# An attention kernel deals its queries to partitions in eights instead of fours

## What is computed

```
x = x + 0.5 * tanh(layernorm(x) @ W @ A1 @ A2 + bias)          # feed-forward
xn = layernorm(x) * ln_g + ln_b
q, k, v = xn @ Wq + bq, xn @ Wk + bk, xn @ Wv + bv             # (8, 1024, 16, 16)
p = pe @ Wp                                                    # (1024, 16, 16)
content = einsum("bihd,bjhd->bhij", q + u_bias, k)
pos     = einsum("bihd,jhd->bhij",  q + v_bias, p)
pos     = relative_shift(pos)     # pad one zero column, view (S+1, S), drop the first row
attn    = softmax((content + pos) * 16 ** -0.5)
x = x + einsum("bhij,bjhd->bihd", attn, v) @ Wo + bo
x = x + 0.5 * tanh(layernorm(x) @ W @ A1 @ A2 + bias)          # feed-forward
```

## Time and profile before

| what | us |
| --- | --- |
| median of 3 runs (lowest to highest) | 3821.3 (3819.82 to 3822.86) |
| the profiled execution, its own time | 3820.24 |
| its span, first to last instruction | 3818.5 |
| attention phase, first to last start of L724 | 518.8 to 3569.0 |
| PE busy, ACT busy, DVE busy, POOL busy | 3384.0, 2312.8, 1830.7, 1265.6 |
| bytes moved by DMA, mean rate | 1221.6 MB, 320 GB/s |

### The profile page before, as it was taken

How to read it: one execution, slowest core, us unless ns; L and a number is a source line. 1 busy time by engine, 2 the same in 40 slices (tenths; PEclk the granted TensorE clock), 3 DMA queues, 4 the chain that set the end, 5 groups by cost and what they waited for, 6 DMA issues and landing times. The chain is left out here.

```text
span 3818.5 us, 86185 instructions
## 1 busy us (share of the span) xinstructions
PE 3384.0 (89%) x24380; PEld 1856.3 (49%) x24380; DVE 1830.7 (48%) x3584; ACT 2312.8 (61%) x3252; POOL 1265.6 (33%) x1228
## 2 busy tenths in 40 slices
PE   3677579999999999999999999999999999999776
PEld 2445334444444444444444444444444444444565
DVE  3555324444444444444444444444444444444444
ACT  1222247666777666667677677666776667776322
POOL 1111023333333333333333333333333333333100
PEclk7888879999999999999999999999999999999888
DMA  2332489999999999999999999999999999999543
GB/s 82 110 110 96 161 283 376 374 374 373 375 375 371 375 372 370 372 373 375 372 376 374 373 373 373 376 374 374 374 374 371 375 374 374 374 375 376 163 115 88
DMA packets 467980, 1221.60 MB, mean 320 GB/s; under 512 B 92144, under 2 KB 176624, under 8 KB 467952
## 3 DMA queue, kind: packets, MB, share of 16 engines
q1 hardware_dynamic: 467952, 1221.25, 88.5%
HBM read 624.38 MB, written 596.65 MB: 320 GB/s over the span
## 5 line engine op out<-in xcount | busy, mean ns | idle before, releaser
L724 DVE CUSTOM_DVE_ANT_0 at_pos_in<-at_ps_con,at_pos_in 128x1024 f32<-128x1024 f32 x1024 | 1254.0, 1225 | 1606.4 <-PE at_ps_con L612 1425.8
L761 POOL TENSOR_SCALAR at_pos_in<-at_pos_in,at_neg_max 128x1024 f32<-128x1024 f32 x1024 | 1146.3, 1119 | 1908.1 <-DVE at_neg_max L724 1908.1
L692 ACT ACTIVATE at_pos_out<-at_ps_pos 128x1024 f32<-128x1024 f32 x1024 | 1049.4, 1025 | 629.8 <-PE at_ps_pos L612 629.8
L701 ACT ACTIVATE at_prob<-at_ps_turn 128x512 f32<-128x512 f32 x2048 | 1110.6, 595 | 362.2 <-PE at_ps_turn L635 362.2
L612 PE MATMUL at_ps_con<-at_right,at_left 32*128 32x512 f32 x4096 | 1156.2, 640 | 153.3 <-DVE at_neg_max L724 151.8
L612 PE MATMUL at_ps_pos<-at_right,at_left 32*128 32x512 f32 x4096 | 1163.8, 644 | 46.9 <-DMA at_right<-scratch_pos_rows 39.0
L635 PEld LDWEIGHTS at_ps_turn<-keep_ident,at_pos_in 128*128 128x128 f32 x8192 | 898.7, 143 | 627.0 <-issue 428.7
L635 PE MATMUL at_ps_turn<-keep_ident,at_pos_in 128*128 128x128 f32 x8192 | 1113.7, 279 | 1.4 <-POOL at_pos_in L761 0.2
L647 PE MATMUL at_ps_pv<-at_prob,at_v_aug 128*32 128x512 f32 x4096 | 545.3, 605 | 0.8 <-issue 0.8
L612 PEld LDWEIGHTS at_ps_con<-at_right,at_left 32*128 32x128 f32 x4096 | 308.2, 183 | 344.9 <-ACT at_pos_out L692 198.8
L658 PEld LDWEIGHTS at_ps_head<-keep_fold,at_head_T 128*128 128x128 f32 x2048 | 247.8, 191 | 195.7 <-DVE at_head_T L732 148.6
(11 more groups left out here) (82 smaller groups left out, 1357.6 us busy)
## 6 DMA issues: line engine op xcount, KB each, us to landing
scratch_scores<-at_pos_out SPq DMA_DIRECT2D x1024, 512.0 KB, 7.5
at_pos_in<-scratch_scores SPq DMA_DIRECT2D x1024, 512.0 KB, 7.7
at_left<-scratch_qk_rows SPq DMA_DIRECT2D x512, 64.0 KB, 5.2
scratch_qk_rows<-de_qk SPq DMA_DIRECT2D x48, 512.0 KB, 5.0
de_x<-in_L_attn_x_dram SPq DMA_DIRECT2D x16, 512.0 KB, 6.4
scratch_x<-de_x_bo SPq DMA_DIRECT2D x16, 512.0 KB, 3.0
scratch_values<-de_values SPq DMA_DIRECT2D x1, 8192.0 KB, 30.3
at_right<-scratch_pos_rows SPq DMA_DIRECT2D x256, 32.0 KB, 5.7
```

Of the source, the lines that this page charges most:

```text
L692: act.activation(pos_out[:, t.slot, :], ps_pos[:, :, :].rearrange("p a m -> p (a m)"), ACT.Copy)\
L701: act.activation(prob[t.t // QUAD % 2][:, 4 * n:4 * n + 4, k * P:(k + 1) * P], ps_turn[:, n, :].rearrange("p (j i) -> p j i", i=P), ACT.Exp)\
L724: dve.tensor_tensor_reduce(pos_in[:, t.slot, :], ps_con[:, :, :].rearrange("p a m -> p (a m)"), pos_in[:, t.slot, :], -SCALE, 3.0e38, ALU. ...
L761: pool.tensor_scalar(pos_in[:, t.slot, :], pos_in[:, t.slot, :], -1.0, neg_max[:, t.slot:t.slot + 1], ALU.mult, ALU.add).then_inc(shifted, 1)
```

## The change

`GAPS` becomes 8. Partition 8v + h now holds query v + 16h of the tile. The scratch tensors in DRAM hold the same values at the same places as before; only the way to and from partitions differs.

```
 STRIP = 32
-GAPS = 4
+GAPS = 8
 HALF = S // 2
```

## The result

The changed kernel takes 4409.2 us (4395.6 to 4416.8, four runs), the kernel before 3822.1 us beside it. The ratio is 1.153 with a 95% interval of 1.150 to 1.156: 15% slower, 587 us more. The forecast was 4435 us.

What follows compares the result with a forecast made beforehand. PE and its chain were taken to lead, the DMA engines just keeping up. Slower write and read-back add 0.60 us a tile, 614 us over 1024 tiles; with 0.4 us of L374 and 3820.2 us, 4435 us, range 3813 to 5150.

Steps and rivals of the forecast that it cites:

- What bounds before: Attention phase: PE and its chain lead at 2.975 us a tile, and the transfers just keep up.
- The engines have no idle time to use: Attention phase: transfers are always queued and the 16 engines never run dry, so 3% slower transfers find no idle time.
- Rival 1: Write and read-back cost the same in the new shape and PE goes on leading: 3821 us, 3815 to 3829; chance 0.28.
- L374 and the heads: Bias-and-copy of the q's costs 0.4 us more, median within 1150 to 1200 ns; the stores of the heads cost nothing.
- Transfers with an outer size of 16 cost the engines more: Write and read-back in 16 groups of 8: engines get in each other's way, up to 1.46 times as long.
- The terms of the sum: Engine time per tile: 3.04 us now, plus 0.44 for the read-back and 0.17 for the write, together 3.65 us.
- 1.12 for the write and 1.31 for the read-back: Factors on 1.43 us of each engine: smallest of three 64 KB loads for the write, their mean for the read-back.
- the DMA then sets the beat, and nothing hides it: Attention phase: a tile takes 3.58 us, 0.60 us over 2.98, in all 614 us for 1024 tiles.
- The signs named: Attention phase: GB/s from 374 to about 310, share near 1.02, read-back waits from 58.7 us to hundreds, PE's busy share falls.
- landings did not grow to 9 us: Sign for write and read-back: landings go from 7.5 us to 9 or more.

Runs made afterwards that it cites:

- light4: The kernel before with the read-back cut to the first 512 of 1024 columns; 3824.4 us against 3833.9.
- w4r8: The kernel before with only the read-back (with the content q and the heads) going by 16 groups of 8; 3990.1 us against 3833.5.
- extra64: The kernel before with one more write of 64 KB beside each tile's write, into a scratch that nobody reads; 4308.9 us, 475 us more than beside it.
- light8: The changed kernel with the read-back cut to the first 512 of 1024 columns; 4262.1 us.
- w8r4: The kernel before with only the write (and its q with the position bias) going by 16 groups of 8; 4537.2 us, timed again at 4527.7 us, ratio 1.179.
- after_lp: The changed kernel with its loads and the store of the heads issued by POOL instead of SP; 4369.6 us, 1.138 of the kernel before.

## Why the prediction was right, point by point

**What bounds before.** Right. PE's beat was read as 2.975 us and light4, without any wait for transfers, runs at 2.976.

**The engines have no idle time to use.** Right. In w4r8 a slower read-back made the tile 0.16 us longer with the share still at 1.02 and SP not full, so nothing hid it. Rival 1 falls with it, and with the write alone at 1.89 us. extra64, made for this point, did not settle it.

**L374 and the heads.** Right: 1167 ns, and the dense phase did not move.

**Transfers with an outer size of 16 cost the engines more.** Right, taken from three loads of 64 KB: alone, 16 groups of 8 took 1.95 us of each engine as a write and 2.11 as a read, where 32 groups of 4 took 1.28 and 1.52. The transfers one by one put the cost at the SBUF side and in both directions. That the engines get in each other's way there was my reading, and no run shows it. What rows 16 apart in DRAM cost is not separated for this very shape, but 8 groups of 16, with rows 8 apart, took no more (1.97 and 2.02 us).

**The terms of the sum.** Mis-sized, and in a way that cancelled: that 4435 us came so near to 4409 is luck. The step that took 1.12 for the write and 1.31 for the read-back failed: alone they measure 1.52 and 1.39. In the mix the single edits cost (4281.8 - 519.2) / 1023 - 2.98 = 0.70 us a tile for the write, where 0.17 was forecast, and 0.16 us for the read-back, where 0.44 was (0.43 at a share of 1.02). The reason given, that reading SBUF had no row and so should suffer less, was a choice without evidence. Nor would the true ratios of transfers alone have helped: with 1.52 and 1.39 the same sum gives (3.04 + 1.43 x 0.52 + 1.43 x 0.39) / 1.02 = 4.26 us a tile, some 5130 us, since in the mix the shapes cost less than alone. The sum for both, 3.58 us a tile, met 3.543 only because the two together cost less than the write alone.

**What nobody had in the account: SP.** The prediction named SP's queue nowhere, although it holds all 26 issues of a unit in order. In light8 it is what binds. In the changed kernel SP and the engines are both full (33.2 us of waits for ACT on SP, a share of 1.00 on the engines). So the step "the DMA then sets the beat, and nothing hides it" is half of what the runs show, and a rate that counted the engines alone came out near.

**The signs named.** GB/s went to 314 (about 310 forecast), the share to 1.00, the waits for the read-back to 1670.8 us, PE's busy share fell from 89% to 80%, and the granted clock from 1.00 to 0.97 in the attention phase. One sign failed: landings did not grow to 9 us but stayed at 7.3 us in the median for the write. The likely reason is that SP is held up at the issue, so that the time goes into the issues and not into the landings: in w4r8, where no issue grew, they did reach 9.0 and 9.3 us.

**Open.** Why both shapes together (4409 us) are faster than the write's alone (4528 us). The engines' time for a tile is nearly the same, 1.00 x 3.543 = 3.54 and 0.97 x 3.678 = 3.57 us, so what differs is idle time of the engines, 3% of the tile in w8r4. SP has next to none in either, and its issues of a unit are 1.4 us longer in w8r4, about the 1.1 us by which the unit is longer; so the difference passes through SP's issues. Why these are held up longer when the read-backs are the fast ones, no run tests. Open too is which of SP and the engines would bind the changed kernel if the other were free; after_lp with its loads placed earlier would tell. And open is what exactly an issue waits for when it is held up.

## What to carry to other kernels

A regrouping of rows on the DRAM side of a transfer is not neutral although bytes, rows and instructions stay the same: here the time went with the size of the outermost dimension. For a tile of 128 partitions, 32 and 64 cost the same (3833.9 and 3833.4 us), and 128 no more than 32 in a write alone (1.26 and 1.28 us of each engine); 16 made the kernel 15% longer, and 8 made it 67% longer. And when transfers get slower, look at the durations of the issues on the queue that sends them as well as at the engines' share: here an issue that was held up delayed what stood behind it in the order, also what has nothing to do with the slow transfer (light8 has 1223 ns for a write's issue in the median where light4 has 551, and was 438 us longer at nearly the same share). A transfer measured alone gives the direction and not the size: 1.52 times alone was 0.70 us a tile in one mix and part of 0.56 in another.

## What the runs showed of the hardware that I had not expected

Writes out of SBUF suffer from few neighbouring partitions as loads into it do: from 16 neighbouring partitions, 512 KB took 4.73 us of each engine, against 1.28 from 128; read into them it took 3.82, against 1.52. With 8 groups, a share of 0.54 moved 202 GB/s when many transfers were queued, though one such write alone moved 109 GB/s over 4.80 us. An issue on SP took about 0.55 us in most places and up to 2.8 us in the changed kernel, the long ones right behind a read-back (1.37 us in the median for a write there, 0.57 behind a load or a store). And landings do not tell how slow the transfers are: the write's median was 7.5 us at 374 GB/s, 7.3 at 314 (the change) and 9.0 at 351 (w4r8).
